# Loading and rounding w_proj by groups of four pieces in a cross-attention and ternary FFN kernel

## The reference

```python
q, k, v = x1 @ Wq + bq, x2 @ Wk + bk, x2 @ Wv + bv      # x1, x2: layernorms with gain and bias
attn = softmax(q @ k.T * E ** -0.5)
x = x + (attn @ v) @ Wo + bo

def bitlinear(x, w):                                    # w_fc (2048, 512), w_proj (512, 2048)
    scale = clip(mean(abs(w), axis=1, keepdims=True), 1e-5, None)
    return x @ (clip(round(w / scale), -1, 1) * scale).T
n = layernorm(x)
h = bitlinear(n, w_fc) + gate * (n @ v.T @ fast_b.T @ u.T)
x = x + bitlinear(relu(h) ** 2, w_proj)
```

## Time and profile before

| | us |
|---|---|
| median of three runs | 788.49 (785.8 to 788.85) |
| profiled execution | 787.38 |
| its span, first to last instruction | 785.6 |
| TensorE busy in it | 768.0 |
| VectorE, ScalarE, POOL busy | 547.7, 367.5, 106.4 |
| end of L:0 of body 0, on TensorE | 93.58 |

### The profile page before, as it was taken

The page is one execution under the profiler, slowest core; times in us unless marked ns, Lnnn a source line. Parts: engine busy times, 40 slices in busy tenths (PEclk is TensorE's granted clock), DMA queues, the critical chain, the costliest instruction groups (busy, mean ns, idle before and its releaser), DMA issues.

```text
span 785.6 us, 10582 instructions
## 1 busy us (share of the span) xinstructions
PE 768.0 (98%) x3761; PEld 638.6 (81%) x3761; DVE 547.7 (70%) x1118; ACT 367.5 (47%) x689; POOL 106.4 (14%) x123
## 2 busy tenths in 40 slices
PE   5899999999999999999999999999999999999997
PEld 3568788888888888888888888888888888888886
DVE  4799876767766786768667686768667686656434
ACT  3798655354533544254543544345442645233332
POOL 2111310100312011210302002210201003000001
PEclk9999999999999999999999999999999999999999
DMA  8844251073214422063213432054212530030101
GB/s 236 305 150 159 41 109 41 1 105 70 81 40 58 67 78 95 1 98 69 89 41 47 71 85 71 24 86 62 107 43 31 79 92 1 1 53 1 54 0 55
DMA packets 180553, 56.92 MB, mean 72 GB/s; under 512 B 167666, under 2 KB 168068, under 8 KB 180500
## 3 DMA queue, kind: packets, MB, share of 16 engines
q1 hardware_dynamic: 150368, 51.51, 27.2%
q10 hardware_dynamic: 30132, 4.73, 3.7%
HBM read 27.64 MB, written 8.39 MB: 46 GB/s over the span
## 4 chain that ended last, share of the span: by engine, by line
PE 94%; SPq 2%; ACT 1%; DVE 1%; DMA 1%; issue 1%; DVEq 0%; ACTq 0%
PE H L1347 30%; PE O L1328 29%; PE G L1212 26%; PE H L1353 4%; PE H L1212 2%; DMA Wv_s<-in_L_xattn_Wv_dram 1%; PE O L1397 1%; SPq L517 1%; PE G L1294 1%; PE H L1189 1%; PE H L1196 0%; SPq L575 0%; SPq L553 0%; PE O L1368 0%; ACT Wvo L722 0%
## 5 line engine op out<-in xcount | busy, mean ns | idle before, releaser
L1328 PE MATMUL O<-projT,qbuf 128*128 128x512 f32 x992 | 242.3, 390 | 0.0
L1328 PEld LDWEIGHTS O<-projT,qbuf 128*128 128x128 f32 x992 | 185.1, 188 | 38.0
L776 ACT ACTIVATE rbuf<-H,scf 128x512 f32<-128x512 f32 x128 | 87.4, 683 | 117.7 <-DVE qbuf L1108 67.1
L1347 PE MATMUL H<-even_group,fcT 128*128 128x512 f32 x512 | 127.5, 391 | 0.0
L1347 PE MATMUL H<-odd_group,fcT 128*128 128x512 f32 x512 | 127.4, 391 | 0.0
L1104 DVE TENSOR_TENSOR rbuf<-rbuf 128x512 f32<-128x512 f32 x128 | 92.1, 728 | 50.4 <-ACT rbuf L776 50.1
L784 ACT ACTIVATE qbuf<-rbuf 128x512 fp32r<-128x512 f32 x125 | 78.6, 629 | 94.8 <-PE O L1328 65.1
L1347 PEld LDWEIGHTS H<-odd_group,fcT 128*128 128x128 f32 x512 | 95.4, 188 | 19.3
L1347 PEld LDWEIGHTS H<-even_group,fcT 128*128 128x128 f32 x512 | 95.2, 188 | 19.2
L1108 DVE TENSOR_TENSOR qbuf<-rbuf,qbuf 128x512 fp32r<-128x512 f32 x125 | 86.1, 689 | 33.3 <-ACT qbuf L784 32.6
L1212 PE MATMUL G<-Wvo,tT 128*128 128x512 f32 x270 | 64.8, 390 | 0.1
(11 more groups left out here) (189 smaller groups left out, 989.2 us busy)
## 6 DMA issues: line engine op xcount, KB each, us to landing
xb<-in_x_dram SPq DMA_DIRECT2D x8, 1024.0 KB, 5.0
n_blocks<-n_rows SPq DMA_DIRECT2D x112, 64.0 KB, 2.3
ctxb<-in_ctx_dram SPq DMA_DIRECT2D x8, 768.0 KB, 4.5
n_blocks<-ctxb SPq DMA_DIRECT2D x112, 48.0 KB, 2.1
wring<-in_L_ffn_w_fc_dram SPq DMA_DIRECT2D x16, 256.0 KB, 5.1
wring<-in_L_ffn_w_proj_dram SPq DMA_DIRECT2D x16, 256.0 KB, 3.0
out_dram<-x2a SPq DMA_DIRECT2D x8, 512.0 KB, 2.6
x_blocks<-x_rows SPq DMA_DIRECT2D x56, 64.0 KB, 3.5
```

What stands on the lines that cost most here:

```text
L776: nc.scalar.activation(rbuf[:, j % 2, :], banks[f"H{j % 2}"][:, :], ACT.Relu, scale=scf[:, j:j + 1]).then_inc(relu_made, 1)
L1328: mm = pe.matmul(banks[f"O{t}"][:, :], qbuf[:, j % 2, h, t * P:(t + 1) * P], projT[:, j, :], start=(j == 0 and h == HI), stop=(j == NFF - ...
L1347: pe.matmul(banks[f"H{j % 2}"][:, :], fcT[:, k, j * P:(j + 1) * P], xnT[:, h, k, :], start=(k == 0 and h == HI), stop=False)
```

## The change

The four pieces of w_proj that belong to the same 128 rows are loaded by one transfer of 1 MB (ring:16, 20, 24 and 28) and rounded by one operation of 128x2048 (round:16, 20, 24, 28). Such a load waits until the whole group two before is rounded; abs:j waits for the group's whole transfer (`ring_landed`); the rounding waits for turn:j-5 and counts as four. Pieces of w_fc are handled as before. Three roundings and three transfers per group leave the lists, and all lists of the preparation and of body 0 are laid anew. The sums, scales, turns and stores stay one per piece.

```diff
--- before.py
+++ after.py
@@ -142,24 +142,24 @@
 FIRST_ORDER = {
     "pe": (
-        "up:3 down:0 down:1 up:4 up:5 down:2 t:0 t:1 t:2 up:6 down:3 up:7 s:0 s:1 down:4 s:2 pT:0 down:5 s:3 up:8 "
-        "pT:1 up:9 w:0 down:6 w:1 w:2 down:7 a:0 a:1 a:2 a:3 up:10 down:8 up:11 up:12 down:9 up:13 down:10 up:14 "
-        "down:11 down:12 up:15 down:13 "
+        "up:3 down:0 down:1 up:4 up:5 down:2 up:6 t:0 t:1 t:2 up:7 down:3 s:0 down:4 s:1 s:2 up:8 pT:0 s:3 up:9 pT:1 "
+        "down:5 w:0 w:1 down:6 w:2 up:10 a:0 a:1 a:2 a:3 down:7 up:11 down:8 down:9 up:12 up:13 down:10 up:14 down:11 "
+        "down:12 up:15 down:13 "
     ).split(),
...
     "dve": (
-        "n1raw0 sq:2 n1raw1 sq:3 n1lo0 n1raw2 lo:2 n1raw3 n1lo1 n1lo2 n1lo3 lo:3 sq:4 t:0 n2raw0 n2raw1 n2raw2 n2lo0 "
-        "t:1 lo:4 n2:0 n2lo1 n2lo2 t:2 n2:1 sq:5 lo:5 s:0 sq:6 s:1 n2:2 n2:3 sq:7 s:2 pT:0 lo:6 s:3 xs01+ pT:1 sq:8 "
-        "w:0 lo:7 xs23+ w:1 lo:8 w:2 sq:9 a:0 a:1 nX0 a:2 a:3 nX1 nX2 lo:9 nX3 cs01+ sq:10 sq:11 lo:10 lo:11 sq:12 "
-        "cs23+ lo:12 xraw0 xraw1 xraw2 xraw3 sq:13 sq:14 lo:13 xlo0 lo:14 sq:15 xlo1 xlo2 xlo3 lo:15 "
+        "n1raw0 n1raw1 n1raw2 n1raw3 sq:2 sq:3 lo:2 n1lo0 n1lo1 n1lo2 n1lo3 lo:3 n2raw0 sq:4 n2raw1 n2raw2 t:0 xs01+ "
+        "n2lo0 sq:5 t:1 t:2 n2lo1 lo:4 n2lo2 n2:0 s:0 xs23+ s:1 lo:5 sq:6 s:2 pT:0 s:3 n2:1 n2:2 sq:7 n2:3 pT:1 lo:6 "
+        "w:0 w:1 cs01+ sq:8 lo:7 w:2 cs23+ lo:8 sq:9 a:0 a:1 a:2 a:3 nX0 nX1 nX2 nX3 lo:9 sq:10 lo:10 sq:11 sq:12 "
+        "lo:11 lo:12 xraw0 xraw1 xraw2 sq:13 lo:13 sq:14 xraw3 lo:14 xlo0 xlo1 xlo2 xlo3 sq:15 lo:15 "
     ).split(),
...
@@ -204,40 +204,39 @@
 PROLOGUE = {
     "sp": (
-        "Wq:2 Wq:0 ring:0 Wq:1 bqrow Wk:0 ring:1 Wq:3 Wk:1 Wk:2 g2row x:0 ring:2 lowrank ring:3 ring:4 ring:5 ring:6 "
-        "ring:7 Wv:0 ring:8 ring:9 ring:10 ring:11 ctx:0 ring:12 ring:13 bo ring:14 ring:15 ring:16 ring:17 ring:18 "
-        "ring:19 ring:20 ring:21 ring:22 ring:23 ring:24 ring:25 ring:26 ring:27 ring:28 ring:29 ring:30 ring:31 next "
+        "Wq:3 Wq:0 Wq:1 Wk:1 Wq:2 ring:0 g2row bqrow ring:1 ring:2 ring:3 Wk:0 Wk:2 x:0 lowrank ring:4 ring:5 ring:6 "
+        "ring:7 Wv:0 ring:8 ring:9 ring:10 ring:11 ctx:0 bo ring:12 ring:13 ring:14 ring:15 ring:16 ring:20 ring:24 "
+        "ring:28 next "
     ).split(),
     "pe": (
-        "wqT:0 wqT:1 vecs wqT:2 wqT:3 bq:0 wkT:0 wkT:1 wkT:2 M:0 M:1 n1T:0 turn:0 turn:1 turn:2 wvT:0 wvT:1 turn:3 "
-        "M:2 wvT:2 turn:4 turn:5 n1T:1 wvo:0 n1T:2 wvo:1 n1T:3 wvo:2 turn:6 turn:7 turn:8 turn:9 n2T:0 n2T:1 turn:10 "
-        "turn:11 co:0 n2T:2 M:3 n2T:3 turn:12 turn:13 fb:0 turn:14 turn:15 t:0 t:1 t:2 turn:16 turn:17 turn:18 "
-        "turn:19 s:0 s:1 s:2 turn:20 turn:21 turn:22 pT:0 s:3 ut:0 ut:1 ut:2 pT:1 ut:3 w:0 w:1 w:2 turn:23 turn:24 "
-        "turn:25 a:0 a:1 a:2 a:3 turn:26 turn:27 x:0 turn:28 turn:29 x:1 x:2 turn:30 turn:31 x:3 sprow B.L:0 B.up:0 "
-        "B.up:1 B.up:2 "
+        "wqT:0 wqT:1 vecs wqT:2 wqT:3 bq:0 wkT:0 wkT:1 wkT:2 M:0 M:1 turn:0 wvT:0 turn:1 wvT:1 n1T:0 M:2 turn:2 "
+        "turn:3 turn:4 turn:5 wvT:2 n1T:1 turn:6 wvo:0 n1T:2 n1T:3 wvo:1 wvo:2 turn:7 turn:8 n2T:0 turn:9 n2T:1 "
+        "turn:10 turn:11 turn:12 co:0 n2T:2 M:3 n2T:3 turn:13 turn:14 turn:15 fb:0 t:0 t:1 turn:16 t:2 turn:17 "
+        "turn:18 turn:19 s:0 s:1 s:2 pT:0 turn:20 s:3 turn:21 ut:0 pT:1 ut:1 turn:22 w:0 w:1 w:2 ut:2 turn:23 turn:24 "
+        "a:0 a:1 a:2 ut:3 a:3 turn:25 turn:26 turn:27 x:0 turn:28 turn:29 turn:30 x:1 turn:31 x:2 sprow x:3 B.L:0 "
+        "B.up:0 B.up:1 B.up:2 "
     ).split(),
     "act": (
-        "wqT:0 vecs abs:0 wqT:2 wqT:3 abs:1 tb Wo abs:2 M:0 abs:4 nx0 abs:5 M:1 abs:6 wvT:0 store:0 wvT:1 nx1 nx2 "
-        "store:1 M:2 n1T:0 abs:8 abs:9 abs:10 wvT:2 store:2 abs:12 nx3 store:3 n1T:1 wvo:0 store:4 abs:13 nc0 n1T:2 "
-        "abs:14 store:5 wvo:1 nc1 abs:16 n1T:3 abs:17 wvo:2 store:6 store:7 n2T:0 nc2 store:8 n2T:1 nc3 store:9 "
-        "abs:18 n2T:2 store:10 M:3 n2T:3 store:11 abs:20 store:12 abs:21 abs:22 fb:0 store:13 store:14 store:15 t:0 "
-        "uhi abs:24 t:1 abs:25 abs:26 t:2 n2:0 store:16 n2:1 store:17 abs:28 n2:2 store:18 s:0 store:19 s:1 store:20 "
-        "s:2 pT:0 store:21 n2:3 store:22 s:3 ut:0 pT:1 abs:29 ut:1 abs:30 w:0 w:1 ut:2 w:2 store:23 nx0+ ut:3 "
-        "store:24 diag nx1+ nx2+ store:25 store:26 store:27 nx3+ store:28 x:0 x:1 x:2 store:29 x:3 B.L:0 store:30 "
-        "store:31 B.up:0 nc0+ B.hi:0 sprow_out B.up:1 nc1+ nc2+ nc3+ B.hi:1 "
+        "wqT:0 vecs abs:0 wqT:2 wqT:3 abs:1 abs:2 tb Wo abs:4 abs:5 M:0 abs:6 M:1 nx0 wvT:0 store:0 store:1 wvT:1 "
+        "n1T:0 nx1 abs:8 M:2 store:2 nx2 store:3 wvT:2 n1T:1 nx3 abs:9 abs:10 store:4 wvo:0 n1T:2 abs:12 abs:13 "
+        "abs:14 nc0 store:5 n1T:3 nc1 wvo:1 store:6 nc2 wvo:2 store:7 store:8 n2T:0 n2T:1 store:9 nc3 store:10 n2T:2 "
+        "abs:16 abs:17 store:11 M:3 n2T:3 store:12 abs:18 store:13 fb:0 abs:20 abs:21 abs:22 t:0 uhi store:14 "
+        "store:15 store:16 t:1 t:2 n2:0 abs:24 n2:1 abs:25 abs:26 n2:2 store:17 s:0 s:1 n2:3 s:2 pT:0 store:18 "
+        "store:19 abs:28 s:3 store:20 abs:29 pT:1 ut:0 ut:1 store:21 abs:30 store:22 w:0 w:1 w:2 nx0+ nx1+ ut:2 nx2+ "
+        "store:23 diag ut:3 nx3+ store:24 store:25 store:26 x:0 store:27 store:28 store:29 x:1 store:30 x:2 store:31 "
+        "x:3 nc0+ nc1+ nc2+ B.L:0 B.up:0 B.up:1 B.hi:0 sprow_out nc3+ B.hi:1 "
     ).split(),
     "dve": (
-        "wqT:1 bqacc bq:0 wkT:0 wkT:1 wkT:2 xs01 xs23 abs:3 M:0 invert:0 round:0 abs:7 round:1 round:2 M:1 invert:1 "
-        "round:3 round:4 round:5 round:6 coacc M:2 round:7 n1T:0 abs:11 cs01 invert:2 cs23 round:8 round:9 n1T:1 "
-        "wvo:0 round:10 round:11 abs:15 n1T:2 invert:3 wvo:1 round:12 n1T:3 round:13 wvo:2 n2T:0 round:14 round:15 "
-        "co:0 abs:19 n2T:1 uprep invert:4 n2T:2 M:3 n2T:3 round:16 round:17 abs:23 round:18 residual:0 fb:0 round:19 "
-        "invert:5 residual:1 residual:2 t:0 round:20 round:21 round:22 ulo abs:27 t:1 t:2 round:23 residual:3 "
-        "invert:6 n2:0 s:0 n2:1 s:1 round:24 s:2 round:25 round:26 abs:31 pT:0 s:3 n2:2 n2:3 B.xs01 pT:1 B.xs23 w:0 "
-        "invert:7 round:27 w:1 round:28 w:2 round:29 B.cs01 round:30 a:0 a:1 nX0 a:2 a:3 nX1 nX2 round:31 nX3 x:0 x:1 "
-        "x:2 x:3 B.cs23 B.L:0 B.sq:0 B.lo:0 B.sq:1 B.lo:1 "
+        "wqT:1 bqacc bq:0 abs:3 wkT:0 wkT:1 wkT:2 xs01 invert:0 xs23 round:0 M:0 round:1 round:2 abs:7 M:1 round:3 "
+        "invert:1 round:4 round:5 round:6 round:7 coacc M:2 n1T:0 n1T:1 abs:11 cs01 cs23 wvo:0 invert:2 round:8 "
+        "round:9 round:10 round:11 abs:15 n1T:2 wvo:1 invert:3 n1T:3 round:12 wvo:2 n2T:0 round:13 round:14 round:15 "
+        "n2T:1 co:0 residual:0 abs:19 n2T:2 M:3 n2T:3 uprep invert:4 round:16 residual:1 residual:2 abs:23 t:0 fb:0 "
+        "invert:5 ulo round:20 t:1 t:2 residual:3 abs:27 n2:0 s:0 s:1 n2:1 s:2 n2:2 n2:3 invert:6 pT:0 s:3 round:24 "
+        "B.xs01 pT:1 abs:31 B.xs23 invert:7 w:0 B.cs01 w:1 w:2 round:28 a:0 a:1 nX0 a:2 nX1 a:3 nX2 B.cs23 nX3 x:0 "
+        "x:1 x:2 x:3 B.L:0 B.sq:0 B.lo:0 B.sq:1 B.lo:1 "
     ).split(),
     "pool": (
-        "tb xs23 scale:0 scale:1 scale:2 cs23 scale:3 scale:4 scale:5 scale:6 scale:7 B.xs23 a:0 a:1 a:2 a:3 B.cs23 "
+        "tb scale:0 xs23 scale:1 scale:2 cs23 scale:3 scale:4 scale:5 scale:6 scale:7 B.xs23 a:0 a:1 a:2 a:3 B.cs23 "
     ).split(),
 }
@@ -499,6 +498,11 @@
             return sum(f"abs:{j}" in PROLOGUE[engine] for j in range(pieces))
+        def ring_landed(e, j):
+
+            first = j if j < NFF else j // 4 * 4
+            e.wait_ge(ring_in[first % 8], 16 * (j // 8 + 1))
+
         def squares(b, j):
             if b == NG - 1 and j >= FIRST_LATE:
@@ -512,9 +516,12 @@
         def _(sp):
             def ring_load(k):
-                src = (w_fc.rearrange("(k p) d -> k p d", p=P)[k] if k < NFF
-                       else w_proj.rearrange("(t p) (c d) -> t p c d", p=P, d=D)[(k - NFF) // 4][:, k % 4, :])
-                sp.dma_start(wring[:, k // 4 % 2, k % 4, :], src).then_inc(ring_in[k % 8], 16)
+                if k < NFF:
+                    sp.dma_start(wring[:, k // 4 % 2, k % 4, :], w_fc.rearrange("(k p) d -> k p d", p=P)[k]
+                                 ).then_inc(ring_in[k % 8], 16)
+                else:
+                    sp.dma_start(wring[:, k // 4 % 2, :, :].rearrange("p c d -> p (c d)"),
+                                 w_proj.rearrange("(t p) h -> t p h", p=P)[(k - NFF) // 4]).then_inc(ring_in[k % 8], 16)
             def load_x(b):
@@ -557,7 +564,9 @@
                     sp.dma_start(ctxb[:, :, :].rearrange("p (c t) d -> p c (t d)", c=2), ctx_in[0]
                                  ).then_inc(ctx_in_s, 16)
                 elif kind == "ring":
-                    if n >= 8:
+                    if n >= NFF:
+                        sp.wait_ge(rounded_made, n - 4)
+                    elif n >= 8:
                         sp.wait_ge(rounded_made, n - 7)
                     ring_load(n)
                 elif kind == "bqrow":
```

(24 more changed lines are left out.)

1 line of the change is left out of this document (removed), and 8 rows, old and new, of the table FIRST_ORDER.

## The result

| | before | after |
|---|---|---|
| time, median | 787.9 us (785.0 to 789.1, 6 runs) | 791.5 us (790.7 to 792.7, 6 runs) |
| ratio | | 1.0052, 95% interval 1.0031 to 1.0074 |
| profiled execution, its span | 787.4, 785.6 | 790.7, 788.9 |

The account below looks back on a forecast made before the run. TensorE, busy 768 of 785.6 us, was taken as the bound, with only its waits ahead of B.L:0 movable. 0.65 + 1.06 + 0.3 = +2.0 on 787.38 gave 789.4, stated as 789.5; range 785 to 793.

Parts of the forecast that it names:

- Term A: Preparation, around Wv's landing: n1T:0, turn:1 and turn:2 now stand behind wvT:0, +0.65 us.
- Term B: Scores and softmax, t:2 to w:0: turn:16 moved, waits at pT:0 and pT:1, ut:2 and ut:3 left over; +1.06 us.
- the uts: ut:2 and ut:3, 0.45 us each, still to be done after w:0 begins; +0.90 counted within the scores and softmax.
- Term C: From w:0 to the end of B.L:0: x:1's wait ends, B.cs23 delays nX3 and x:3; +0.3 us without the uts.
- Wide rounding 1.4: VectorE: one 128x2048 rounding takes 1.4 us against 1.6 for four narrow ones, sparing 0.2 per group, 0.8 in all.
- Body 0: 0: Body 0's matmuls run without a gap, so cost 0, kept at 0 to +1 us if cover is gone.
- The bytes ahead of Wv are the same: Early loads on SyncE are only reordered, so Wv's landing, awaited by TensorE at 26.77, was taken as unchanged.
- Wv landing over 1 us earlier or later: One of the listed signs that the prediction is wrong; wvT:0 was expected at 26.3 to 27.
- other rivals: New order closes waits, 785.5 (0.23); clock dip goes, 783.9 (0.1); invert:7 holds VectorE, over 791.3 (0.17).
- The rival in which the dip goes: Waits before Wv no longer lower the clock, M:2 takes 2.75 us: -1.6 more, 783.9; chance 0.1.
- invert:7 as the hold: invert:7, ahead of w:0 on VectorE, waits for scale:7 and delays w:0 to a:0; over 791.3, chance 0.17.

Follow-up runs that it names:

- Wo later: Wo's transfer issued behind M:0 on ScalarE instead of right behind tb: 787.6 us, 0.9997, in the kernel after; 785.35 us, 0.9955, in the kernel before.
- all three put back: Kernel after with Wo issued behind M:0, and softmax fillers, B.cs23 and ScalarE's stores put back as in the kernel before: 788.0 us, ratio 1.0006.
- The old lists: Wide transfers and roundings alone, put into the kernel before's lists of the preparation and body 0: 791.7 us, ratio 1.0048.
- the last experiment: Kernel after, Wo behind M:0, fillers, B.cs23 and stores put back, TensorE's old order from t:2 to B.L:0; edit mistake with n2:3: 791.0 us, 1.0033.

## Why it came out so, point by point

- **Term A, +0.65: measured +0.43**, with a dip in both kernels, and +0.24 with Wo later in both and no dip. Profiles of the same lists differ by more (1.3 us in this stage), so the runs neither confirm nor refute the term. n1T:0 and the turns are behind wvT:0, as said.
- **Term B, +1.06: the order of waits was right, the path behind pT:1 was not.** s:0's wait grew from 0.74 to 0.97, the +0.22 of turn:16. pT:0 has the new wait, 0.32 (0.4 forecast). pT:1's wait was put at 1.1; it is 0.44, and 0.33 more stands ahead of ut:0, for a copy by ScalarE. w:0 came 10.1 us behind t:2, and not 9.97. But what counts is the low half of pT:1 on VectorE, behind round:24, which the term does not have: it sets w:1, 0.45 late against t:0. And of the two uts, put at 0.45 each, ut:2 cost at most the 0.15 behind a:3 and ut:3 0.37.
- **Term C and the uts, +1.2: measured +1.13.** x:1's wait is gone; there is one ahead of x:3 (0.46) and one in B.L:0 (0.78). L:0 ends 32.6 behind t:2's end, where 32.5 was forecast; that parts with other sizes and causes add up so closely is luck. The cause was only half seen: B.cs23 was blamed, and the experiment that moved it alone gained 0.1. ScalarE's stores ahead of x:3's copy hold B.L:0 as well; both together are 0.6. The other 1.0 of the 1.55 that the kernel with Wo later lost between t:0 and the end of B.L:0 remains with all three put back, and the timelines split it: 0.45 up to w:1 by VectorE's low half of pT:1, 0.37 by ut:3, 0.15 behind a:3. B.cs23 was put at 1.65 us; its rows reach from 92.21 to 93.92, 1.71, which changes nothing.
- **Wide rounding 1.4: 1.28 to 1.29**, inside the bounds 1.1 to 1.6, so VectorE is spared 1.3 us by it (4 x 0.32, an estimate from the 1.6 of four in a row) and not 0.8. The Trainium skill ("VectorE: DVE Perf Modes", "Side-by-side: where the cycles go for N=2048 bf16") gives, for bf16, 1.22 us for two elements per cycle at this width; this trace, with f32 in and f16 out, agrees to 0.07. The 1 MB transfers landed after 4.8 us with no wait of ScalarE for them in the new lists. The old lists, and the last experiment, show the price where that cover is gone: a wait of 2.6 and one of 2.15 us. **Body 0: 0**, as said.
- **Where it failed: "The bytes ahead of Wv are the same", and its landing taken as unchanged.** The bytes on SyncE's queue were counted, and not those that ScalarE's queue sends at the same time. tb, and behind it Wo's 1 MB, comes sooner when all of Wq is first; the step of tb and Wo stood in the diff's ScalarE list and was not timed. wvT:0 came 1.29 us later in the profile, and by the medians Wo's place was worth 3.9 us, the clock with it. The prediction did name it as what would make it wrong, "Wv landing over 1 us earlier or later", and Wv landed 1.2 us later. That the time stayed in the range is in part luck: the range was made wide for other rivals, and none of them is this one.
- **The clock.** The rival in which the dip goes did not come with the change: it came with Wo's move, and would have come to the kernel before too. The Trainium skill ("TensorE: Matmul & The Clock Gate", "HAM oscillation — how this bites in real kernels") says that waits for transfers throttle the engine anew; the traces agree, with the fall to 0.50 in or just behind waits of 3.3, 3.6 and 1.9 us, and none behind one of 0.19. The length of the wait alone does not decide it: with three matmuls put ahead, one of 2.74 passed at 1.00.
- **invert:7 as the hold: not seen.** In the kernel after w:0 to w:2 run without a wait.

Shown by runs: with Wo issued ahead of Wv, Wv lands late and the clock dips, and moving Wo takes the whole loss back; the reordering costs 1.57 us between t:0 and the end of B.L:0, of which the stores and B.cs23 are 0.6. Read from the timelines, with no run that moves it alone: the split of the remaining 1.0. Open: what the reordering costs ahead of t:0, if anything.

## What to carry to other kernels

Before taking a transfer's landing as unchanged, list what every queue issues in the microseconds around it, not only its own queue, and time the releaser of each. When a needed transfer is late, first move away the one that is less urgent: issuing Wo behind M:0 was worth 3.9 us in the one kernel and 3.0 in the other (785.35 against 788.3 on the same chip), more than the 2.3 us that the medians give for the whole reordering. Then look who wants the transfer that was moved: here it was coacc, ahead of M:2 in VectorE's list, and it cost up to 1.8 us of TensorE. Whether coacc behind M:2 would save that, no run tells. A filler taken back from one wait gains only if the next stage does not wait for another engine, and to see that, look for waits inside a job and not only ahead of it. And before a difference between two profiles is given a cause, compare profiles of the same lists.

## What the runs showed of the hardware

Where a 1 MB transfer on ScalarE's queue was issued 1.8 us or more behind a 768 KB one on SyncE's queue, the latter landed 6.0 to 7.0 us after its issue; where it was issued level with it or ahead, 8.5 to 10.2 us. With nothing else changed, moving it took the latter from 8.5 to 6.3 in the kernel after and from 7.4 to 6.9 in the kernel before. The clock dip differs from one execution to the next of one kernel: of 30 executions of the kernel before, twelve had a mean granted clock of 0.996 and took 789.4 us in the mean, and the four with 0.999 or 1.0 took 785.3. So a good part of a spread of 4 us in 788 that looks like noise goes with this dip. It is not all of it: in the kernel after, executions with 0.990 and with 0.998 took 791.5 us alike, and with Wo later those at 1.0 still span 786.7 to 789.9. A kernel without the wait has less of the dip: 8 of 12 executions at 1.0 with Wo later, against none of 6 in the kernel after.
